# Layer 1 of a graph network: the gathers beside the table copy in twos, paced by TensorE's steps, and another mix of gathers and additions behind it

## The reference

```python
h = relu(layernorm(x))
x_i, x_j = h[dst], h[src]
feat = concat([x_i, x_j - x_i])                 # 512 features an edge
msg = relu(feat @ W1 + b1) @ W2 + b2            # 512 -> 512 -> 256
out = segment_sum(msg, dst) / (degree + 1e-8)
x = x + out
```

## Time and profile before

| | us |
|---|---|
| median of 3 runs | 2254.42 (2254.4 to 2258.35) |
| profiled execution, its own time | 2253.34 |
| span of the profile, first to last instruction | 2251.5 |
| TensorE busy | 1767.0 (78%) |
| VectorE busy | 1496.5 (66%) |
| ScalarE busy | 1034.8 (46%) |
| GpSimd (POOL) busy | 1280.7 (57%) |

### The profile page before, as it was taken

How to read it: one execution, slowest core, us unless ns; L and a number is a source line. 1 busy time by engine, 2 the same in 40 slices (tenths; PEclk the granted TensorE clock), 3 DMA queues, 4 the chain that set the end, 5 groups by cost and what they waited for, 6 DMA issues and landing times.

```text
span 2251.5 us, 46578 instructions
## 1 busy us (share of the span) xinstructions
PE 1767.0 (78%) x14020; PEld 1537.2 (68%) x14020; DVE 1496.5 (66%) x6002; ACT 1034.8 (46%) x2106; POOL 1280.7 (57%) x1024
## 2 busy tenths in 40 slices
PE   7958787886666667303888888889999999989995
PEld 2258777786566667303776776778888888878875
DVE  8969888996666667303555555567777776757573
ACT  0024444453333333203454554556666775656563
POOL 2033332478888788655222222246888888888874
PEclk9989999998878888656998888899999999999998
DMA  8989999566555656457898999623555555545553
GB/s 295 317 294 326 321 338 310 148 112 103 103 102 105 103 101 107 56 106 223 300 297 284 300 300 289 205 70 71 95 95 92 95 96 91 96 90 97 89 89 38
DMA packets 142804, 379.84 MB, mean 169 GB/s; under 512 B 31806, under 2 KB 97353, under 8 KB 129865
## 3 DMA queue, kind: packets, MB, share of 16 engines
q0 software_dynamic: 86400, 131.14, 32.4%
q1 hardware_dynamic: 27452, 208.63, 27.1%
q10 hardware_dynamic: 28912, 39.64, 6.6%
HBM read 325.72 MB, written 259.17 MB: 260 GB/s over the span
## 4 chain that ended last, share of the span: by engine, by line
POOL 16%; PE 15%; issue 13%; another core or an unknown queue 4%; ACT 3%; DVE 3%; DMA 1%; ACTq 1%; DVEq 0%; POOLq 0%
PE ps_h L1224 9%; POOL table_out L932 9%; POOL ends L920 7%; PE ps_m L1238 2%; PE ps_s L1251 2%; DVE e_moments L974 1%; PE ps_t L1211 1%; ACT feat_hi L1130 1%; ACT hid L1137 1%; ACT ends L1123 1%; DVE out_sum L1046 1%; DVE feat_lo L1041 1%; DMA table_out<-e_ring,e_targets_all 1%; ACT e_ring L1155 0%
## 5 line engine op out<-in xcount | busy, mean ns | idle before, releaser
L920 POOL DMA_INDIRECT ends<-x,keys x400 | 399.8, 1000 | 436.2 <-PE ps_t L1211 312.3
L772 PE MATMUL ps_deg<-table,hot 128*128 128x128 bf16 x5600 | 357.9, 225 | 75.6 <-issue 66.8
L1224 PE MATMUL ps_h<-feat_hi,w_hi 128*128 128x512 f32 x800 | 337.1, 421 | 94.2 <-ACT hid L1137 77.8
L772 PEld LDWEIGHTS ps_deg<-table,hot 128*128 128x128 bf16 x5600 | 334.7, 101 | 94.1 <-issue 82.6
L465 POOL DMA_INDIRECT x<-sums_ring,targets_all x200 | 329.2, 1646 | 88.8 <-issue 65.0
L932 POOL DMA_INDIRECT table_out<-e_ring,e_targets_all x200 | 328.6, 1643 | 86.3 <-issue 58.7
L455 POOL DMA_INDIRECT rows<-in_x,row_idx x200 | 208.7, 1043 | 243.9 <-ACT normed L699 190.1
L1224 PE MATMUL ps_h<-feat_lo,w_hi 128*128 128x512 f32 x800 | 330.4, 413 | 0.0
L1224 PE MATMUL ps_h<-feat_hi,w_lo 128*128 128x512 f32 x800 | 329.2, 412 | 0.0
L786 PE MATMUL ps_sum<-msg_hi,same 128*128 128x260 f32 x800 | 154.9, 324 | 155.3 <-issue 148.9
L1224 PEld LDWEIGHTS ps_h<-feat_hi,w_hi 128*128 128x128 f32 x800 | 159.8, 200 | 147.8 <-ACT hid L1137 89.2
(11 more groups left out here) (141 smaller groups left out, 3538.6 us busy)
## 6 DMA issues: line engine op xcount, KB each, us to landing
table_out<-x SPq DMA_DIRECT2D x400, 252.0 KB
x<-in_x SPq DMA_DIRECT2D x400, 250.0 KB
hi_row<-hi_rows ACTq DMA_DIRECT2D x50, 256.0 KB
src_row<-src_rows ACTq DMA_DIRECT2D x50, 256.0 KB
dst_row<-dst_rows ACTq DMA_DIRECT2D x50, 256.0 KB
ends<-x,keys POOLq DMA_INDIRECT x400
rows<-in_x,row_idx POOLq DMA_INDIRECT x200
x<-sums_ring,targets_all POOLq DMA_INDIRECT x200
```

The source lines that it names most:

```text
L772: last = nc.tensor.matmul(ps_deg[q][k][:, j * P:(j + 1) * P], hot[:, c, k, j * P:(j + 1) * P], table[:, c, part, :], start=(c == 0 and par ...
L920: pool.indirect_dma_start(out=ends[b % NE][:, n, :], out_offset=None, in_=x1_d, in_offset=bass.IndirectOffsetOnAxis(ap=keys[:, 1 - end, at ...
L1224: last = nc.tensor.matmul(ps_h[m % 2][:], w[:, k, m * P:(m + 1) * P], f[:, k, :], start=(k == 0 and n == 0), stop=(k == KF - 1 and n == 2))
```

## The change

The lead becomes 20 batches. Within the lead, a wait stands ahead of every second gather (`pace`): batch 1 waits until batch 0 has landed, batch 2 for the landing of batch 1, for transpositions of batch 0 and for the first mm1_done; from batch 3 on, the four pairs of a batch wait for the second and fourth mm1_done and for both mm2_done of TensorE's step b-3. Behind the copy the additions have eleven gathers to four pairs (2, 3, 3, 3) instead of five to two (2, 3), for 240 gathers instead of 224.

```diff
-    LEAD1 = 22
+    LEAD1 = 20
...
+                def pace(b, n):
+                    if b == 1 and n == 0:
+                        pool.wait_ge(ends_in[0], 16 * 2 * W)
+                    elif b == 2:
+                        if n == 0:
+                            pool.wait_ge(ends_in[1], 16 * 2 * W)
+                        elif n < 6:
+                            pool.wait_ge(turned, n)
+                        else:
+                            pool.wait_ge(mm1_done, 1)
+                    elif b >= 3:
+                        if n < 4:
+                            pool.wait_ge(mm1_done, KH * (b - 3) + 2 + n)
+                        else:
+                            pool.wait_ge(mm2_done, GROUPS * (b - 3) + n // 2 - 1)
+
                 for b in range(LEAD1):
                     for n in range(2 * W):
+                        if n % 2 == 0:
+                            pace(b, n)
                         gather(b, n)
...
-                    for n in range(min(left, 5 * c // 2), min(left, 5 * (c + 1) // 2)):
+                    for n in range(min(left, 11 * c // 4), min(left, 11 * (c + 1) // 4)):
```

## The result

The changed kernel takes **2146.44 us** (median of 4 runs, 2139.8 to 2149.3) against 2254.41 us of before (4 runs, 2253.12 to 2258.35) on the same chip: ratio **0.951**, 95% interval 0.9492 to 0.9528, 4.9% faster. The forecast was 2198 us with a range of 2182 to 2222: the direction is right, the gain is almost twice the forecast (108 us for 56). And one thing that the forecast had no place for came out in the experiments: on four other chips the kernel before takes only 2125 to 2135 us, and on the two of them on which the changed kernel ran beside it, the change makes it *slower*, by 0.7 and 0.8%.

The account below looks back on a forecast made before the run. GpSimd's stream of additions, its start and length, was taken to set the end. First addition at 1448 us plus 747 us of stream gave a 2195 us span and a 2198 us forecast; range 2182 to 2222 us.

Parts of the forecast that it names:

- What bounds the kernel: Layer 1: when GpSimd's stream of additions starts and how long it is set the end; 734.8 us from first addition.
- The gaps come from bursts, and pairs are too short for them: Lead beside the copy: eight queued gathers hold all engines; two plus 2.2 us make 4.7 us, little above 4 us tolerated.
- The step: TensorE's step beside the copy: 21.5 us instead of 27.8, with bounds 20.47 and 27.8 us.
- When the copy ends: Layer 1: copy's end stays at 1446 us, first addition at about 1448 us, bounds 1439 and 1453.
- Step 16 ends at 1402, well before the copy: Lead: step 16, awaited by the last two lead gathers, ends at 1402 us, so the later copy decides the start.
- idle for 30 to 40 us: Sign in the changed profile: TensorE waits some 30 to 40 us for gathers ahead of about 1475 us.
- The stream of 747 us: GpSimd behind the copy: 747 us from first addition to the end, against 734.8 us before.
- The 7.58 us a pair: Pairs of additions with gathers behind the copy: 7.58 us each instead of 7.27, bounds 7.4 and 7.8 us.
- the 6.3 us of the uncovered pairs: Last pairs of additions, without gathers, wait for their own landing: 6.3 us each, eleven of them.
- No late data: Last two gathers of a paced batch have 12.9 us to land and need 9.2 at most; nothing added.
- Rival 1: Beside the copy: gaps stay, step 27.8 us, 2262 us, 0.3% slower, chance 0.06; start alone saved, 2250 us, 0.03.

Follow-up runs that it names:

- The kernels in fours and eights: The changed kernel with each batch's gathers, from batch 3 on, in two bursts of four (2169.36 us) or one burst of eight (2259.6 us).
- the memsets: The kernel before with 128 memsets without waits ahead of VectorE's first work of layer 1: 2276.32 us on chip 0, 2127.35 us on chip 9.
- the two versions with the short stream: Changed kernel, paced earlier: lead 21 with thirteen gathers to five pairs (1.0019, 1.0041, 1.0027 of before); lead 22 with five to two (1.005, 1.0039).

## Why the prediction was right or wrong

1. **What bounds the kernel** (the start and the length of GpSimd's stream): right. 122.5 us of earlier start less 13.5 us of longer stream is the whole gain of 109 us.
2. **The gaps come from bursts, and pairs are too short for them**: right in the mechanism. The step was put at 21.5 us and is 20.5. The kernels in fours and eights show it as a matter of the run's length. Two details don't hold: the memsets ran on for 9 us of the burst at the start, not some 4, and slowed down until 6 us behind its end, not 2.2. And a third of what a gap cost was TensorE's lower clock after it, which the prediction has inside the 27.8 us of its step and doesn't name.
3. **"When the copy ends": the step that failed.** The term had the copy's end at 1446 and the first addition at 1448 us; measured 1394.20. I took the 295 GB/s of before as what the DMA engines can give beside gathers, and only added bytes to it. The rows had the contrary in them: a DMA share of 0.90 in the earlier trace rows is a tenth idle, and the fall to 153 GB/s under the 32 gathers was read there as part of the hold, but was priced only for these 30 us. A hold in every burst costs the copy, too: at 333 GB/s the 128.6 MB of copy, 20 batches of gathers and row loads take 386 us and end at 1390. The kernel with large pieces shows it apart: same bursts, no idle DMA engine, 345 GB/s. With 1394 in place of 1448 the sum gives 2144 us.
4. **Step 16 ends at 1402, well before the copy**: it ends at about 1391. TensorE began it all at 1041.76 instead of 1037 us, but 17 steps at 20.5 instead of 21.5 us gave 16 us back. That this falls together with a copy that is quicker than I thought is luck: with the 21.5 us of the forecast step 16 would have ended at 1407 us, 15 us behind the copy, and the lead would have decided. It does so as it is, by 1.5 us (1393.90 against 1392.35). TensorE never stood idle for 30 to 40 us as foretold.
5. **The stream of 747 us**: 748.3. The 7.58 us a pair and the 6.3 us of the uncovered pairs both held: 2059.10 for pair 88 is 664.9 us after the first addition (666 forecast), and eleven more take 70.8 us (69.3).
6. **No late data**: right for this copy. The kernel with 512 KB pieces and pairs shows the same margin used up.
7. **Rival 1** (the gaps stay, slower by 0.3%) did not come, but its other half is real: where there are no gaps to remove, the longer stream is all that is left. 748.3 against 733.5 us of stream is 15 us, and the first addition comes 394 us after the first gather of layer 1 in the kernel before and 393 us after it in the changed one: 0.7 and 0.8% slower on two chips. I had read the gap as a property of the program. It is one of the program on a certain chip.

**What stays open.** What makes the holds. They were on chips 0 and 4 and on that of the first pair of profiles. On chip 9 the profile of the kernel before has none, and its times of 2125 to 2135 us on chips 2, 10 and 12 say the same of those. Each chip was used at one or two times only, so it may also be a state of the machine at that hour. All times come from executions that were also traced, so whether an untraced execution shows the holds isn't known. Why the engines get one instruction in 0.7 or 1.4 us is open as well: it touches memsets without a semaphore and register operations of SP, which speaks against late semaphores and against the transfers. The Trainium skill ("Runtime: NRT & Kernel Launch", Instruction fetch mechanics) has instructions fetched in blocks through a DMA queue. I would expect late blocks to make single long gaps, not an even 1.4 us, so the memsets don't bear that out. Nor does the DMA view of the kernel before: from 1190 to 1250 us, with VectorE's gaps of 7.95 and 3.53 us, it lists no packet of an instruction queue, and 8 from 1060 to 1430 us. The Trainium skill's rule on arbitration ("DMA: Bandwidth & Descriptors", Queues, rings and completion order) agrees as far as transfers go: large copy pieces kept 345 GB/s beside bursts, and gathers and copy shared full DMA engines. The changed kernel itself ran on one chip with holds only; the pacing alone did so on a second one, chip 4. And the two versions with the short stream have not run on a chip with holds; that their earlier pairs stay free of holds there is likely from the step times of pairs, but not shown.

## What to carry to other kernels

When one queue issues a long run of indirect DMAs, look at the others' gaps: if they end with the run and name no engine, split the run into twos before touching anything else, and look at SP, too, since a copy may be slow only because its issuer is held. A DMA share below 1 beside a copy (0.90 here) says that the DMA engines were not what limited it: price a change that frees the issuer at the rate of full DMA engines with the gathers beside (334 GB/s here), not at the rate of the copy alone. Count what TensorE's clock loses after each gap, too. And run before and after on several chips: a gain that comes from removing a hold is only there where the hold is, while the price (here 15 us of longer stream) was paid on the chips without it as well; of the versions that ran, the one with a lead of 21 and thirteen gathers to five pairs costs the least (0.2 to 0.4%) where there is nothing to gain.

## What the runs showed of the hardware that I had not expected

- While gathers were queued without a pause, on some chips, VectorE issued one memset in 0.7 or 1.4 us instead of one in 0.14, and SP's register operations took up to 1.5 us instead of 0.03 to 0.05. TensorE's matmuls of 512 columns went on at one in 0.23 us, until they needed a result of ScalarE.
- After 6.1 us without work TensorE ran at a granted clock of 0.50 for another 6 us; this was 2.6 of the 7.8 us that a step lost.
- The same program took 2254 us on some chips and 2125 to 2135 us on others, with equal durations of gathers and additions. The mean granted clock was 0.896 against 0.908; beside the copy it was 0.88 against 1.00, since only where there were gaps did it fall.
- A copy from DRAM to DRAM moved 312 GB/s alone. With paced gathers of 1 KB rows beside it all traffic together was 334 GB/s, 270 of them the copy; in pieces of 512 KB the sum was 345 to 351, and there paced gathers came late.
